# First four tiles mixed on 64x64 fourths of TensorE, first-stage products in groups of two and four blocks over several tiles, first loads issued from three queues

## The chip, the cores and the metric

The kernel runs on one core of a Trainium2 chip. The metric is the time of one execution on the device in microseconds (us). A core has five engines with queues of their own, each strictly in order, that meet only at semaphores: TensorE (PE in the profile, with PEld for its weight loads), VectorE (DVE), ScalarE (ACT), GpSimd (POOL) and SyncE (SP), which here only issues transfers. ACT and POOL can issue transfers too. PSUM, the memory that TensorE writes, cannot be read by POOL.

## The reference, cut to what matters

x is 32 x 64 x 1024 in f32. There are two layers, each a mix of the 64 channels of every batch entry by a matrix picked from a table, and then a 1024 x 1024 product over the last axis:

```
W = weights[condition]                      # 32 matrices of 64 x 64, picked from 16
y = einsum('bct,bcd->bdt', x, W)            # the mix over channels
x = x + y @ (w + (ternary(w) - w)) + b      # layer 0; ternary(w) = (|w| < 0.05 ? 0 : sign(w)) * mean|w| of a column
y = einsum('bct,bcd->bdt', x, weights1[condition])
x = x + y @ dequantized(q).T + bias + 4 * (y @ A.T) @ B.T     # layer 1; 4-bit levels, a scale for each 64
```

The output is x after both layers.

## The kernel before

**Tiles.** Two batch entries make a tile of 128 rows (2 x 64 channels) by 1024 columns: 16 tiles, `g` = 0 to 15 in layer 0, and the same 16 again as `g` = 16 to 31 in layer 1. The 1024 columns are 8 blocks `k` of 128 (`KB`), or two halves `n` of 512 (`BANK`).

**Work on a tile in layer 0.** PE mixes and turns the tile in one step, with x as the stationary operand: block k of x (128 rows by 128 columns) against the tile's two 64 x 64 matrices, which stand in `mix` as a block-diagonal 128 x 128 (`mixed(g)`), or on fourths of the array, 64 x 64 each, which skips the zero corners (`mixed_batches(g)`, tiles 4 to 15). The result goes to the PSUM tensor `xT` or, for tiles 1 and 3, to the banks 2 and 3 of `acc`. ACT rounds it into a high part (`high_x(g, h)`, tensor `hh` or `h23`, semaphore `s_hh`) and DVE takes the rest as a low part (`low_x(g, h)`, `hl` or `h23`, `s_hl`). PE then multiplies both parts by the ternary signs `T0` and accumulates 8 blocks x 2 parts into a bank of `acc` (`first(g, n, h)` for the tiles 0 to 3, in halves of four blocks, `main(g, n)` for the tiles 4 to 15). DVE scales the bank by the column means (`leave_y`, tensor `ys`), and POOL adds it to x (`result_half`, `result`), after `add_bias`. `ys` has four places, so `leave_y(q)` waits until POOL has finished `result_half(q - 4)` (`s_res0`).

**The signs.** For each of 16 pieces (n, k) of the first weight, 128 x 512, the signs are made either by ACT (`signs`, into `spare`, then `absolute` in place) with one DVE instruction (`ternary`), or by two DVE instructions (`ternary` of the blocks 0, 1, 4 and 6 of the first half), after which ACT still does `absolute`. `s_T0` counts the finished pieces. POOL adds up the absolute values of 8 pieces for each half with 7 additions, in the order of `ABS` (`sums(0, ...)`: 2, 3, 0, 1, 5, 4, 7, 6; then `sums(1, ...)`: 0 to 7). PE spreads each sum with a product of ones (`column_sums(n)`) and ACT scales it (`colscale(n)`).

**What sets the order.** All orders are written out by hand, for each engine a list of calls. POOL's list starts with the two `sums`, then alternates `add_bias(g)` and `result_half`, with `weight(d)` (a part of layer 1's weights) in between. DVE and ACT make layer 1's weights meanwhile (`maxima`, `lines`), 16 pieces `d` spread over the tiles 4 to 15, which PE turns (`turn_w`). After tile 15 come 8 pairs of tiles of layer 1 (`product`, seven products for each pair).

**Loads.** SP issues nearly all. Each 64 x 64 matrix for `mix` is one transfer whose address is looked up in `tok`. ACT issues the second matrices of the tiles 0 to 2 and the pieces 0 and 2 of the weight; POOL issues none.

The lists that the change touches begin like this on PE and on ACT:

```
turn_b()  mixed(0)  mixed(1)  mixed(2)  first(0, 0, 0)  first(1, 0, 0)  mixed(3)
first(0, 0, 1)  first(1, 0, 1)  column_sums(0)  first(2, 0, 0) ...
```

```
high_x(0)  signs(0, 2)  absolute(0, 2)  signs(0, 3)  absolute(0, 3)  high_x(1)
absolute(0, 0)  absolute(0, 1)  high_x(2) ... absolute(0, 7)  high_x(3)  absolute(0, 6)  signs(1, 0) ...
```

## Time and profile before

| | before |
|---|---|
| median of 3 runs | 343.64 us (343.38 to 344.93) |
| the profiled execution, its own time | 344.56 us |
| its span (first to last instruction) | 342.5 us |
| PE busy | 332.4 us, 97% |
| DVE busy | 236.0 us, 69% |
| POOL busy | 245.0 us, 72% |
| ACT busy | 164.5 us, 48% |

The span runs over three stages: the start until `main(4, 0)` at 51.0 us, the tiles 4 to 15 of layer 0 until 170.8 us, and layer 1. All views below have their times in us from the start of the span, so the difference of 2.1 us between time and span lies outside of them. A matmul of f32 operands leaves two records in the trace, one of fp32r operands leaves one.

### The profile page before, as it was taken

The page shows a single profiled execution, that of the slowest core. Times are in us where ns is not written, and L with a number is a line of the kernel's source. Part 1 is how long each engine was busy: PE and PEld are TensorE (multiplying, and loading weights), DVE is VectorE, ACT ScalarE, POOL GpSimd, SP SyncE. Part 2 cuts the span into 40 slices and gives each one's busy share as a digit, 9 for nine tenths or more (in the row PEclk, how much of TensorE's full clock was granted, in tenths as well). Part 3 has the DMA queues.
Part 4 walks back from the last instruction along what each step waited for, and adds up shares of the span by engine and source line. Part 5 has one row for each costly group of instructions (what it writes and reads, how often), then busy time and mean ns, then how long its engine had stood idle before and what let it go on. Part 6 is the DMA issues. An engine that isn't in the chain of part 4 may idle for free.

```text
span 342.5 us, 8187 instructions
## 1 busy us (share of the span) xinstructions
PE 332.4 (97%) x3142; PEld 271.4 (79%) x3142; DVE 236.0 (69%) x356; ACT 164.5 (48%) x300; POOL 245.0 (72%) x160
## 2 busy tenths in 40 slices
PE   7999999989999999999799999999999999999996
PEld 6868778778888778887678888888888888888884
DVE  7787567899999999999999736346263462624623
ACT  1799357877897787788171403214032140411400
POOL 0298999998896896986578966766467664677642
PEclk9999999999999999999999999999999999999999
DMA  6894511644354245300100151412513124150302
GB/s 229 291 341 132 201 33 33 271 168 159 118 167 162 93 157 177 141 10 13 55 2 3 65 189 63 150 44 74 181 65 131 63 84 169 67 169 23 124 31 92
DMA packets 25800, 40.60 MB, mean 119 GB/s; under 512 B 7810, under 2 KB 16002, under 8 KB 25762
## 3 DMA queue, kind: packets, MB, share of 16 engines
q1 hardware_dynamic: 25090, 39.48, 33.3%
q10 hardware_dynamic: 672, 0.61, 0.5%
q8 instruction: 25, 0.41, 0.5%
q14 instruction: 13, 0.11, 0.1%
HBM read 25.40 MB, written 14.68 MB: 117 GB/s over the span
## 4 chain that ended last, share of the span: by engine, by line
PE 51%; DVE 20%; POOL 12%; issue 8%; ACT 4%; DMA 1%; SPq 1%; DVEq 0%; POOLq 0%; ACTq 0%
PE acc L1268 45%; POOL col_scale L631 4%; DVE hl L914 3%; DVE ys L941 3%; POOL x_first L604 3%; PE spare L1154 2%; PE xT L1154 2%; POOL x_first L611 2%; DVE side_n L953 2%; ACT spare L762 2%; DVE W L988 2%; DMA w_in<-in_L_ffn_w 1%; POOL side_p L638 1%; DVE side_p L953 1%; DVE side_n L956 1%
## 5 line engine op out<-in xcount | busy, mean ns | idle before, releaser
L1268 PE MATMUL acc<-W,hh 128*128 128x512 f32 x256 | 81.4, 389 | 0.0
L1228 PE MATMUL acc<-T,hh 128*128 128x512 f32 x192 | 76.5, 398 | 0.0
L1228 PE MATMUL acc<-T,hl 128*128 128x512 f32 x192 | 75.0, 391 | 0.0
L604 POOL TENSOR_TENSOR X<-X,bias 128x1024 f32<-128x1024 f32 x28 | 68.1, 2432 | 0.0
L762 ACT ACTIVATE spare<-q_raw 128x512 f32<-128x512 int32 x96 | 56.1, 599 | 20.2 <-DVE side_n L953 5.0
L1040 DVE TENSOR_TENSOR X<-X,acc 128x512 f32<-128x512 f32 x48 | 32.9, 685 | 36.7 <-PE acc L1268 28.9
L1268 PEld LDWEIGHTS acc<-W,hh 128*128 128x128 f32 x256 | 48.0, 188 | 10.0
L663 POOL TENSOR_TENSOR X<-X,ys 128x512 f32<-128x512 f32 x24 | 30.5, 1299 | 34.1 <-DVE ys L1029 34.1
L1268 PE MATMUL acc<-W,hl 128*128 128x512 f32 x128 | 49.8, 389 | 0.0
L797 ACT ACTIVATE hh<-xT 128x512 fp32r<-128x512 f32 x16 | 8.7, 595 | 77.6 <-PE xT L1154 77.6
L1228 PEld LDWEIGHTS acc<-T,hh 128*128 128x128 f32 x192 | 36.0, 188 | 8.0
L1228 PEld LDWEIGHTS acc<-T,hl 128*128 128x128 f32 x192 | 36.1, 188 | 7.3
L1029 DVE TENSOR_TENSOR ys<-acc,ys 128x512 f32<-128x512 f32 x16 | 11.0, 690 | 34.2 <-PE acc L1268 33.3
L617 POOL TENSOR_TENSOR X<-X,ys 128x1024 f32<-128x1024 f32 x12 | 29.3, 2438 | 2.8 <-DVE ys L941 2.7
L638 POOL TENSOR_TENSOR side_p<-side_p,side_n 128x512 f32<-128x512 f32 x16 | 20.8, 1299 | 13.4 <-DVE side_n L959 13.4
L1268 PEld LDWEIGHTS acc<-W,hl 128*128 128x128 f32 x128 | 24.0, 188 | 5.0
L654 POOL TENSOR_TENSOR side_S<-plain_sums,side_S 128x512 fp32r<-128x512 f32 x8 | 10.4, 1302 | 23.0 <-ACT side_S L814 23.0
L941 DVE TENSOR_TENSOR ys<-acc,col_scale 128x512 f32<-128x512 f32 x32 | 21.8, 683 | 3.7 <-POOL x_first L611 3.7
L1268 PE MATMUL acc<-W 128*128 128x512 f32 x96 | 24.0, 399 | 0.0
L1268 PE MATMUL acc<-W,side_S 128*128 128x512 f32 x96 | 23.2, 390 | 0.0
L1268 PE MATMUL acc<-W_T,W 128*128 128x512 f32 x96 | 23.1, 389 | 0.0
L654 POOL TENSOR_TENSOR hl<-plain_sums,hh 128x512 fp32r<-128x512 f32 x16 | 21.6, 1353 | 0.0
(98 smaller groups left out, 606.5 us busy)
## 6 DMA issues: line engine op xcount, KB each, us to landing
out<-X SPq DMA_DIRECT2D x22, 512.0 KB, 3.1
X<-in_x SPq DMA_DIRECT2D x12, 512.0 KB, 3.4
X<-out SPq DMA_DIRECT2D x12, 512.0 KB, 3.8
q_raw<-in_L_ffn_q_weight SPq DMA_DIRECT2D x16, 256.0 KB, 2.9
w_in<-in_L_ffn_w SPq DMA_DIRECT2D x14, 256.0 KB, 6.8
x_first<-in_x SPq DMA_DIRECT2D x4, 512.0 KB, 5.1
out<-x_first SPq DMA_DIRECT2D x4, 512.0 KB, 4.6
out<-X SPq DMA_DIRECT2D x4, 256.0 KB, 2.0
```

The lines of the kernel that those rows point to most:

```text
L604: pool.tensor_tensor(x_of(g), x_of(g), bias[:, :], ALU.add).then_inc(s_xb, 1)
L617: pool.tensor_tensor(x_of(g), x_of(g), ys[:, at:at + NH, :].rearrange("p a f -> p (a f)"), ALU.add).then_inc(s_res0, NH)
L631: pool.tensor_tensor(col_scale[:, cols], col_scale[:, cols], w_raw(ABS[n][j], n), ALU.add).then_inc(s_sum, 1)
L638: pool.tensor_tensor(lev, lev, side_n[:, :], ALU.subtract).then_inc(s_lev, 1)
L654: pool.tensor_tensor(side(o, 1).rearrange("p b c -> p (b c)"), plain(i), side(o, 0).rearrange("p b c -> p (b c)").bitcast(F32), ALU.subtra ...
L663: pool.tensor_tensor(t, t, sum_of(which), ALU.add).then_inc(s_sum2, 1)
L762: act.activation(dst, q_raw[:, d % QS, :, :].rearrange("p o i -> p (o i)"), ACT.Copy, scale=slope, bias=offset).then_inc(s_line, 1)
L941: dve.tensor_tensor(ys[:, q % F, :], acc[:, bank_of(q), :], col_scale[:, n * BANK:(n + 1) * BANK], ALU.mult).then_inc(s_ys, 1)
L1040: dve.tensor_tensor(t, t, bank, ALU.add).then_inc(s_take, 1)
L1154: mm = pe.matmul(turned(g, h)[c * C:(c + 1) * C, k, rows], x_of(g)[rows, at:at + C], mix[rows, g % NM, rows], start=True, stop=True)
L1228: mm = pe.matmul(acc[:, bank_of(q), :], a[:, k, :], T0[:, n, k, :], start=(k == 0 and j == 0), stop=(k == KB - 1 and j == 1))
L1268: mm = pe.matmul(acc[:, bank, :], a[:, k, :], w1(part, c, k), start=(k == 0 and j == 0), stop=(k == HB - 1 and j == len(terms) - 1))
```

## The change

It reworks the lists of the start; everything from `main(4, 0)` on is the same.

1. The tiles 0 to 3 are mixed by `mixed_batches` too; tile 1 goes to the banks 2 and 3 of `acc`, the tiles 0, 2 and 3 to `xT`. The semaphore `s_xT` then rises by 2 at the end of a tile, not by 1 at each half. `high_x` and `low_x` work on columns for each batch entry instead of on blocks.
2. `first(g, n, start, stop)` takes a range of blocks, and PE's list interleaves ranges of 2 and 4 blocks of the tiles 0 to 2.
3. `idle(products)`: 7 products of the identity ahead of `turn_b` instead of 5, 4 after it, and 2 ahead of tile 1.
4. The second half of `loraB` is copied by ACT instead of DVE; ACT does `high_x(1)` ahead of `signs(0, 3)`, DVE does `low_x(1)` ahead of `ternary(0, 2)` and `low_x(2)` ahead of `ternary(0, 4)`.
5. POOL issues the weight pieces 0 and 1 and the four matrices of the tiles 2 and 3 (with semaphores of their own) ahead of its sums; ACT issues only the second matrices of the tiles 0 and 1; SP the rest.

```diff
-    WARM = 5
+    WARM = 7
@@ turned, batch
-            if g in (1, 3):
-                return acc[:, 2 + h, :].rearrange("p (b c) -> p b c", b=HB)
+            if g == 1:
+                return acc[:, 2 + s, :].rearrange("p (k c) -> p k c", k=KB)
@@ sync
             load_condition(sp, 0, 0)
             load_condition(sp, 1, 0)
+            load_weights(sp, 2, 0)
             load_x(2)
-            load_condition(sp, 2, 0)
-            load_weights(sp, 1, 0)
             load_weights(sp, 3, 0)
-            load_condition(sp, 3, 0)
             load_weights(sp, 4, 0)
+            load_weights(sp, 5, 0)
             load_x(3)
-            load_condition(sp, 3, 1)
-            load_weights(sp, 5, 0)
@@ gpsimd
+            load_weights(pool, 0, 0)
+            load_weights(pool, 1, 0)
+            pool.wait_ge(s_tok, 16)
+            pool.wait_ge(s_fill, 1)
+            for g in (2, 3):
+                for s in range(2):
+                    load_condition(pool, g, s)
             sums(0, 1, KB)
             sums(1, 1, KB)
@@ scalar
             load_condition(act, 0, 1)
-            load_weights(act, 0, 0)
             load_condition(act, 1, 1)
-            load_weights(act, 2, 0)
-            load_condition(act, 2, 1)
+            act.wait_ge(s_bT, 2)
+            act.activation(lora_columns(1), lora_turned(1), ACT.Copy).then_inc(s_loraB, 1)
             high_x(0, 0)
             high_x(0, 1)
             signs(0, 2)
             absolute(0, 2)
+            high_x(1, 0)
+            high_x(1, 1)
             signs(0, 3)
             absolute(0, 3)
-            high_x(1, 0)
-            high_x(1, 1)
@@ vector
+            dve.wait_ge(s_bT, 1)
+            dve.tensor_copy(lora_columns(0), lora_turned(0)).then_inc(s_loraB, 1)
             ternary(0, 0)
             low_x(0, 0)
             low_x(0, 1)
             ternary(0, 1)
+            low_x(1, 0)
+            low_x(1, 1)
             ternary(0, 2)
             ternary(0, 3)
-            low_x(1, 0)
-            low_x(1, 1)
+            low_x(2, 0)
+            low_x(2, 1)
             ternary(0, 4)
-            low_x(2, 0)
             ternary(0, 5)
-            low_x(2, 1)
@@ tensor
-            def first(g, n, h):
+            def first(g, n, start, stop):
 
                 q = n * F + g
-                if h == 0:
+                if start == 0:
                     bank_free(pe, q)
                     if q < NH:
-                        pe.wait_ge(s_loraB, q + 1)
-                    if g == 2:
-                        pe.wait_ge(s_hl, NH * F)
-                pe.wait_ge(s_hl, NH * g + h + 1)
-                for k in range(h * HB, (h + 1) * HB):
+                        pe.wait_ge(s_loraB, NH)
+                    pe.wait_ge(s_hl, NH * max(g + 1, 2 if q in (2, 3) else 0))
+                for k in range(start, stop):
                     pe.wait_ge(s_T0, n * KB + k + 1)
...
+            idle(WARM)
             turn_b()
-            mixed(0)
-            mixed(1)
-            mixed(2)
-            first(0, 0, 0)
-            first(1, 0, 0)
-            mixed(3)
-            first(0, 0, 1)
-            first(1, 0, 1)
+            idle(4)
+            mixed_batches(0)
+            idle(2)
+            mixed_batches(1)
+            first(0, 0, 0, 2)
+            first(1, 0, 0, 2)
+            mixed_batches(2)
+            first(0, 0, 2, 4)
+            first(1, 0, 2, 4)
+            first(2, 0, 0, 4)
+            first(0, 0, 4, 6)
+            mixed_batches(3)
+            first(1, 0, 4, 6)
+            first(2, 0, 4, 6)
+            first(0, 0, 6, KB)
+            first(1, 0, 6, KB)
+            first(2, 0, 6, KB)
+            first(3, 0, 0, HB)
             column_sums(0)
-            first(2, 0, 0)
-            first(2, 0, 1)
-            first(3, 0, 0)
-            first(3, 0, 1)
-            first(0, 1, 0)
-            first(0, 1, 1)
-            first(1, 1, 0)
+            first(3, 0, HB, KB)
+            first(0, 1, 0, HB)
+            first(1, 1, 0, HB)
+            first(0, 1, HB, KB)
+            first(1, 1, HB, KB)
             column_sums(1)
```

On PE, from `turn_b` (b_wide) on, this stood before, where `s_hl` counts low parts, `s_T0` finished sign pieces, and tile 0 multiplies four blocks in a row:

```order
L1284 MATMUL acc<-ident,b_wide 128x128 x7
L1139 MATMUL xT<-mix,x_first 128x128 [waits s_x00,s_mix0]
L1139 MATMUL xT<-mix,x_first 128x128 x7
L1139 MATMUL acc<-mix,x_first 128x128 [waits s_x01,s_mix1]
L1139 MATMUL acc<-mix,x_first 128x128 x7
L1139 MATMUL xT<-mix,x_first 128x128 [waits s_hl,s_x02,s_mix2]
L1139 MATMUL xT<-mix,x_first 128x128 x7
L1216 MATMUL acc<-T,hh 128x512 [waits s_T0,s_hl,s_loraB]
```

And this stands there now, up to the mixing of tile 2:

```order
L1299 MATMUL acc<-ident 128x128 x4
L1169 MATMUL xT<-mix,x_first 64x64 [waits s_x00,s_mix0]
L1169 MATMUL xT<-mix,x_first 64x64 x31
L1299 MATMUL acc<-ident 128x128 x2
L1169 MATMUL acc<-mix,x_first 64x64 [waits s_x01,s_mix1]
L1169 MATMUL acc<-mix,x_first 64x64 x31
L1211 MATMUL acc<-T,hh 128x512 [waits s_T0,s_hl,s_loraB]
L1211 MATMUL acc<-T,hl 128x512
L1211 MATMUL acc<-T,hh 128x512 [waits s_T0]
L1211 MATMUL acc<-T,hl 128x512
L1211 MATMUL acc<-T,hh 128x512 [waits s_T0,s_hl,s_loraB]
```

The mixing of tile 2 has moved behind two blocks of products of each of the tiles 0 and 1.

On ACT, from the high parts of tile 0 (`hh<-xT`) on, before:

```order
L723 ACTIVATE hh<-xT 128x512 [waits s_xT] x2
L730 ACTIVATE spare<-w_in 128x512 [waits s_T0,s_win2]
L736 ACTIVATE w_in<-w_in 128x512 [waits s_sign]
L730 ACTIVATE spare<-w_in 128x512 [waits s_T0,s_win3]
L736 ACTIVATE w_in<-w_in 128x512 [waits s_sign]
L723 ACTIVATE hh<-acc 128x512 [waits s_xT] x2
```

And now, where the signs of piece 3 (`s_win3`), whose absolute value is the second that POOL's sums wait for, stand behind the high parts of tile 1 (`hh<-acc`):

```order
L739 ACTIVATE hh<-xT 128x8x64 [waits s_xT] x2
L746 ACTIVATE spare<-w_in 128x512 [waits s_T0,s_win2]
L752 ACTIVATE w_in<-w_in 128x512 [waits s_sign]
L739 ACTIVATE hh<-acc 128x8x64 [waits s_xT] x2
L746 ACTIVATE spare<-w_in 128x512 [waits s_T0,s_win3]
L752 ACTIVATE w_in<-w_in 128x512 [waits s_sign]
```

On POOL, ahead of the first sum, stand now two weight loads and four matrices, of which the first is shown; before, the sums followed the identity directly:

```order
L489 DMA w_in<-in_L_ffn_w 128x512 x2
L481 TENSOR_LOAD tok [waits s_fill,s_tok]
L481 ISA x2
L483 ISA
L483 DMA mix<-in_L_cond_weights 64x64
```

## Rows read from the trace of the kernel before

**Rows 1.** Page, busy time by engine, and granted TensorE clock in 40 slices.
```profile
PE 332.4 (97%) x3142; PEld 271.4 (79%) x3142; DVE 236.0 (69%) x356; ACT 164.5 (48%) x300; POOL 245.0 (72%) x160
PEclk9999999999999999999999999999999999999999
```

**Rows 2.** Chain that ended last, in order of time: start, length, what.
```profile
6.82 5.10 DMA w_in<-in_L_ffn_w
...
14.10 0.63 ACT w_in L736
...
16.30 1.31 POOL col_scale L631
...
64.95 1.27 POOL side_p L638
66.24 0.63 ACT side_n L762
```

**Rows 3.** Timeline of POOL: start, length, line, what, idle before and releaser.
```profile
14.81 1.29 POOL L627 TENSOR_TENSOR col_scale<-w_in 128x512 f32<-128x512 f32 x1 [13.33 <-ACT w_in L736]
...
24.83 1.28 POOL L627 TENSOR_TENSOR col_scale<-w_in 128x512 f32<-128x512 f32 x1
...
33.45 2.10 POOL L631 TENSOR_TENSOR col_scale<-col_scale,w_in 128x512 f32<-128x512 f32 x1
35.51 2.41 POOL L604 TENSOR_TENSOR x_first<-x_first,bias 128x1024 f32<-128x1024 f32 x1
...
51.53 2.55 POOL L611 TENSOR_TENSOR x_first<-x_first,ys 128x512 f32<-128x512 f32 x2
```

**Rows 4.** Timeline of DVE, same columns.
```profile
11.95 0.69 DVE L929 TENSOR_SCALAR spare<-w_in 128x512 f32<-128x512 f32 x1 [0.39 <-DMA w_in<-in_L_ffn_w]
...
15.36 1.28 DVE L918 TENSOR_TENSOR hl<-acc,hh 128x512 fp32r<-128x512 f32 x2
...
33.14 1.25 DVE L1083 TENSOR_TENSOR loraA<-a_in,loraA 64x1024 fp32r<-64x1024 f32 x1 [0.26 <-ACT loraA L872]
...
52.95 0.69 DVE L941 TENSOR_TENSOR ys<-acc,col_scale 128x512 f32<-128x512 f32 x1 [3.66 <-POOL x_first L611]
...
67.39 0.69 DVE L953 SCALAR_TENSOR_TENSOR side_n<-side_n,spare 128x512 f32<-128x512 f32 x1 [0.83 <-ACT spare L762]
```

**Rows 5.** Busy time in 51 to 171 us; then PE's timeline at its longest wait there.
```profile
51.00:171.00 120.00, 115.91 (x1238) 93.35 (x1234) 111.37 (x170) 90.64 (x169) 99.33 (x60) 1.00 0.36 123
...
164.82 0.63 PE L1296 MATMUL acc<-ident,side_p 128*128 128x128 f32 x4 [1.86 <-DVE W_sums L978]
```

**Rows 6.** Timeline of TensorE's weight loads at the start.
```profile
1.53 2.21 PEld L1303 LDWEIGHTS acc<-ident 128*128 128x128 f32 x10 [1.53 <-POOL ident L667]
4.52 1.57 PEld L1284 LDWEIGHTS acc<-ident,b_wide 128*128 128x128 f32 x8 [0.78 <-DVE b_wide L1054]
6.42 3.48 PEld L1139 LDWEIGHTS xT<-mix,x_first 128*128 128x128 f32 x16 [0.34 <-DMA mix<-in_L_cond_weights]
...
11.96 1.87 PEld L1139 LDWEIGHTS xT<-mix,x_first 128*128 128x128 f32 x16
```

**Rows 7.** Timeline of PE: column sums 0; tile 5 mixed on fourths, then tile 4.
```profile
24.82 1.12 PE L1277 MATMUL xT<-col_scale,ones 128*128 128x512 f32 x2
25.38 7.86 PE L1216 MATMUL acc<-T,h 128*128 128x512 f32 x32
...
49.90 1.16 PE L1172 MATMUL xT<-mix,X 64*64 64x64 f32 x64
50.99 0.50 PE L1228 MATMUL acc<-T,hh 128*128 128x512 f32 x1
```

**Rows 8.** Timeline of ACT.
```profile
14.63 1.07 ACT L723 ACTIVATE hh<-acc 128x512 fp32r<-128x512 f32 x2
...
21.81 0.63 ACT L736 ACTIVATE w_in<-w_in 128x512 f32<-128x512 f32 x1
22.33 0.60 ACT L730 ACTIVATE spare<-w_in 128x512 f32<-128x512 f32 x1
...
26.96 0.58 ACT L740 ACTIVATE col_scale<-xT 128x512 f32<-128x512 f32 x1
```

**Rows 9.** Timeline of SP's queue, ACT's queue and DVE in the first microseconds.
```profile
3.08 0.58 SPq L467 DMA_DIRECT2D mix<-in_L_cond_weights  x1
4.45 0.47 SPq L467 DMA_DIRECT2D mix<-in_L_cond_weights  x1
...
2.79 0.91 DVE L1044 MEMSET a_in<- 128x1024 f32 x1 [0.16 <-DVE ones L1044]
```

74 lines of the change are left out of this document (30 added, 44 removed).

## Prediction

> **What bounds the kernel now.** The page comes first. PE is busy for 97% of the span at the full granted clock [rows 1], which invites the reading that every microsecond taken from PE is gained. The chain that ended last says otherwise for the first half: it leaves the start with a weight transfer, DVE and ACT, and enters POOL's first sums at about 16.3 us; it stays on POOL until 66.2 us and then on ACT and DVE [rows 2]. POOL's timeline shows why. Its first sum starts at 14.81, after a wait of 13.33 for ACT's `absolute`; from then on one instruction follows another: 14 sums at 1.44 us from start to start ((24.83 - 14.81)/7 = 1.43), the last one 2.10 long, then from 35.51 the pairs of `add_bias` and `result_half`, up to `result_half(3)`, the first of the two at 51.53 [rows 3]. DVE waits 3.66 us for exactly that one, at 52.95, and later only 0.83 at 67.39 [rows 4]; from 51 to 171 it is busy 111.4 of 120 us while PE, busy 115.9, waits 1.86 for DVE at 164.82 [rows 5]. So PE has some 4 us of idle time in that stretch, and it is DVE, released at 52.95 by POOL, that sets the end of layer 0. The rest is PE's own and is not touched. The question for the change is therefore when POOL finishes the second sums (35.51 before), not when PE reaches `main(4, 0)` (50.99 before [rows 7]).
>
> **The change, step by step.** Times are positions in the trace.
>
> *Tile 0 mixed, t0.* The 5 warm-up products take 0.44 each (2.21/5), `turn_b` 1.57 [rows 6]. Seven end at 1.53 + 7 x 0.44 = 4.6, which closes the pause ahead of `turn_b` (b_wide was ready at 4.5) and costs 0.1; `turn_b` ends at 6.2. A product of this size takes 0.44 at first (3.48/8) and 0.23 later (1.87/8) [rows 6], the two levels of the clock (1.2 and 2.4 GHz), although the page grants the full clock throughout [rows 1]. Before, the change of rate lies inside tile 1, between 10 and 12 us, and PE had paused at 3.7 to 4.5 and at 6.1 to 6.4. Now neither pause exists, so I let the rate change at about 7: four idle products end at 7.5. A tile on fourths takes 1.09 (49.90 to 50.99 [rows 7], whatever the change of shape costs included) against 1.9 to 3.5 whole. The matrices and x had landed by 6.42, where PE waited for them [rows 6]; with two more 256 KB loads in flight I allow 7.5. So t0 = 8.6. Bounds: 7.5 (6.42 + 1.1, rate changed early) and 10.2 (idle until 8.0, the tile twice as long).
>
> *The first signs.* `high_x(0)` 1.07 [rows 8], DVE's low parts end at t0 + 2.0, `ternary(0, 1)` needs 1.4 (two of 0.69 [rows 4]), so two pieces are signed at 12.0; before, this step waited for its weight until 11.95 and was done at 13.4. `signs(0, 3)` and `absolute(0, 3)` take 1.3 and POOL could start at 13.4, 1.4 us earlier than before.
>
> *The new waits.* `low_x(1)` now follows (1.2, a pair is 1.28 [rows 4]): 13.2. PE's list has `first(1, 0, 0, 2)` ahead of tile 2, so tile 2 is mixed from 13.2 + 0.9 = 14.1 to 15.2. Its high parts end at 16.4 and its low parts, which DVE now does ahead of `ternary(0, 4)`, at 17.2: DVE stands still from 14.4 to 16.0. `ternary(0, 4)` and `(0, 5)` end at 18.65 and 19.25. PE needs both for `first(0, 0, 4, 6)`, which stands ahead of tile 3: tile 3 is mixed from 20.1 to 21.2, and `high_x(3)`, ahead of `absolute(0, 6)` on ACT, ends at 22.3. `absolute(0, 6)` ends at 22.9, against 22.44 before (21.81 + 0.63), and `signs(1, 0)` starts at 22.85 against 22.33 [rows 8]. The lead of 1.4 us is a lag of 0.5 here: what tile 3's mixing gates on ACT has been put behind DVE's signs.
>
> *Second sums.* Each sign and absolute of the second half costs ACT 1.155 (four from 22.33 to 26.96 [rows 8]). `absolute(1, 1)` ends at 25.2, POOL's second sums start at 25.3 (24.83 before). Then ACT comes to `colscale(0)` at 27.5. PE's `column_sums(0)` stands behind 28 products of 0.2275 (7.86 for 32 gives 0.24 with the last one's own length; starts are 0.2275 apart) after tile 3: 27.6, ready at 28.2 with half of the 1.12 for the two passes. Before, it was done at 25.4, ahead of ACT's 26.96 [rows 7, 8]. ACT waits 0.75, the absolute of the fifth piece ends at 30.1, POOL would have wanted it at 29.6, and the last sum starts at 34.45. It ends at 35.75 if it takes the usual 1.30 and at 36.55 if it takes 2.10 as the last one did [rows 3] beside DVE's `loraA` correction (33.14, 1.25 long [rows 4]), which now falls on it again. Against 35.51 that is +0.2 to +1.0; I take +0.6.
>
> A rule bears on which. By the Trainium skill (SBUF — State Buffer, Who interferes with whom) a DVE instruction with two inputs in SBUF and a reading GpSimd instruction exclude each other, and whoever starts first keeps the ports. The trace agrees: DVE's correction starts first and ends at 33.14 + 1.25 = 34.39, and the sum beside it ends 1.16 later. By it POOL, starting 0.1 us ahead here, would take 1.30, DVE would pay, and the sum would be +0.2; by the row it is +1.0.
>
> *Loads on POOL.* No row shows POOL issuing. Nearest are SP's: a matrix with its look-up every 1.37 (3.08 to 4.45) and about 0.5 for a plain one [rows 9]: 2 x 0.5 + 4 x 1.37 = 6.5, done at 8.0. At twice that it is done at 14.5. Seven sums need 10.1 and the second sums cannot start before 25.3, so POOL may start as late as 15.2 at no cost; the loads are hidden in both cases. At three times, POOL would start at 21 and end near 42. SP and ACT shed four look-ups and two weight loads between them; this brings the later pieces earlier, but only piece 1 (0.39 [rows 4]) and, shortly, piece 2 had been waited for, and the new lists reach both later than they land.
>
> *After the sums.* POOL's list is unchanged and every input of it is ready earlier than needed, so the +0.6 goes to DVE at 52.95, on to 164.8 and to the end. PE reaches `main(4, 0)` at about 47.5: four tiles on fourths save about 5, eight idle products and its waits until 20 give back the rest. The 3.4 us go into longer waits for DVE.
>
> Sum: span 342.5 + 0.6 = 343.1. The profiled execution took 344.56, 0.9 above the median of the runs; against that median (343.64) the forecast is 344.2.
>
> **Rivals.** *PE bounds after all.* Then the 3.4 us of its lead arrive at the end: 340.2. For it: 97%. Against: DVE's 111 of 120 busy us and PE's wait at 164.82 [rows 5], and DVE can't move without POOL. A part of this case is also that I have a wait of the start too long, so that POOL ends 2 us earlier: 341.6. Together 0.17.
>
> *The rate of TensorE changes no earlier than before.* t0 = 10.2, tile 1 is mixed at 11.9, `low_x(1)` ends at 14.9 instead of 13.2, and every step behind it moves by 1.7: 345.9. For it: the page can't tell when it changes; against: PE has no pause. It decides from t0 = 9.7 on (over half a percent slower). 0.14.
>
> *POOL's own loads land late.* Piece 0 must be there by 7.9, or `low_x(0)` waits for `ternary(0, 0)` (1.4). Were POOL held back until DVE's memsets end at 3.70 [rows 9] and the load took the 5.10 of piece 1's [rows 2], it would land at 8.8 to 9.3: +1.0 to +1.4 on every step, 345.4. 0.11.
> The Trainium skill (DMA: Bandwidth & Descriptors, SWDGE vs HWDGE vs iDMA) speaks for this rival: transfers from GpSimd have their descriptors made in software, and a DVE instruction that holds the shared ports starves it. No row here shows it.
>
> *Forecast,* 0.58: POOL's end moves by -0.3 (t0 = 7.6) to +1.2.
>
> **Numbers.** Half a percent, 1.7 us, is about what a measurement here tells from no change. Faster by more: 0.17, the first rival. Slower by more: most of the second and over half of the third, and a tail of the forecast: 0.22. Same: 0.61. The range 341.5 to 346.3 leaves out the better half of the first rival and the ends of the slow ones; the forecast's own range is 343.3 to 344.9.
>
> **What would show it.** Right: POOL's first sum near 13.4 but its second sums at 25.3 and `add_bias(0)` near 36; ACT waiting for PE ahead of `colscale(0)`; DVE idle ahead of tile 2's low parts, near 15; PE's `main(4, 0)` near 47.5 with more idle time from 51 to 171; DVE's wait at 52.95 longer, its end at 53.5. Wrong: `add_bias(0)` before 34; PE's products at 0.44 beyond 9; a first sum after 15.2; or a DVE that no longer waits for POOL at 53.

## Result and the profile after

| | before | changed |
|---|---|---|
| time, median of 5 runs | 343.96 us (343.38 to 345.14) | 348.09 us (347.06 to 348.70) |
| profiled execution: time, span | 344.56, 342.5 us | 348.48, 346.8 us |
| mean granted TensorE clock in it | 0.999 | 0.990 |

The changed kernel is 4.1 us slower by the medians. By the means it takes 1.0107 times as long (95% interval 1.0073 to 1.0140), which is 3.7 us. The forecast of 344.2, and its range up to 346.3, are missed on the slow side.

First TensorE's weight loads, in the timeline of the changed kernel (as in [rows 6]; columns of all timelines are start, length, engine, line, what, and idle before with its releaser):

```profile
5.90 0.97 PEld L1299 LDWEIGHTS acc<-ident 128*128 128x128 f32 x8
8.56 1.02 PEld L1169 LDWEIGHTS xT<-mix,x_first 64*64 64x64 f32 x64 [1.69 <-DMA mix<-in_L_cond_weights]
9.66 0.52 PEld L1299 LDWEIGHTS acc<-ident 128*128 128x128 f32 x4
```

Its products (as in [rows 7]):

```profile
15.44 1.16 PE L1169 MATMUL xT<-mix,x_first 64*64 64x64 f32 x64
...
21.59 1.16 PE L1169 MATMUL xT<-mix,x_first 64*64 64x64 f32 x64
...
29.17 1.02 PE L1272 MATMUL xT<-col_scale,ones 128*128 128x512 f32 x2
```

ACT (as in [rows 8]):

```profile
22.82 1.09 ACT L739 ACTIVATE h<-xT 128x512 fp32r<-128x512 f32 x2 [0.95 <-PE xT L1169]
23.79 0.63 ACT L752 ACTIVATE w_in<-w_in 128x512 f32<-128x512 f32 x1
24.31 0.60 ACT L746 ACTIVATE spare<-w_in 128x512 f32<-128x512 f32 x1
...
30.22 0.60 ACT L756 ACTIVATE col_scale<-xT 128x512 f32<-128x512 f32 x1 [1.19 <-PE xT L1272]
```

PE has its full rate early (the 4 idle products behind `turn_b`, 8 records, in 0.97 us), but then waits 1.69 us for the matrix of tile 0, and tile 0 is mixed at 9.66. The chain that ended last shows that matrix from its issue by SP to its landing at 8.53 (start, length, what):

```profile
3.23 5.30 DMA mix<-in_L_cond_weights
```
Tile 2 is mixed from 15.44, tile 3 from 21.59, the signs of the second half start at 24.31, and ACT waits 1.19 us for the first column sums.

POOL of the changed kernel (as in [rows 3]):

```profile
14.48 1.29 POOL L640 TENSOR_TENSOR col_scale<-w_in 128x512 f32<-128x512 f32 x1 [6.69 <-ACT w_in L752]
...
26.81 1.29 POOL L640 TENSOR_TENSOR col_scale<-w_in 128x512 f32<-128x512 f32 x1 [1.01 <-ACT w_in L752]
...
32.06 5.62 POOL L644 TENSOR_TENSOR col_scale<-col_scale,w_in 128x512 f32<-128x512 f32 x4 [1.10 <-ACT w_in L752]
37.64 3.37 POOL L617 TENSOR_TENSOR x_first<-x_first,bias 128x1024 f32<-128x1024 f32 x1
```

DVE (as in [rows 4]):

```profile
17.30 1.29 DVE L928 TENSOR_TENSOR h<-xT,h 128x512 fp32r<-128x512 f32 x2 [1.87 <-ACT h L739]
...
36.42 2.33 DVE L1090 TENSOR_TENSOR loraA<-a_in,loraA 64x1024 fp32r<-64x1024 f32 x1 [0.26 <-ACT loraA L887]
...
56.01 0.69 DVE L950 TENSOR_TENSOR ys<-acc,col_scale 128x512 f32<-128x512 f32 x1 [4.78 <-POOL x_first L624]
```

POOL starts its second sums at 26.81 (24.83 before) and `add_bias(0)` at 37.64 (35.51), which takes 3.37 us instead of 2.41. DVE is released at 56.01 instead of 52.95 [rows 4]: 3.06 us later. The parts add up: 1.98 (start of the second sums) + 0.15 (their length) + 0.96 (the longer `add_bias(0)`) = 3.09. PE reaches `main(4, 0)` at 50.76, where the prediction had 47.5 and before it was 50.99, so PE has next to no lead.

The rest of the 4.3 us of span shows in PE's later timeline:

```profile
56.85 1.09 PE L1291 MATMUL acc<-ident,side_p 128*128 128x128 f32 x4 [2.17 <-DVE ys L950]
...
167.82 0.63 PE L1291 MATMUL acc<-ident,side_p 128*128 128x128 f32 x4 [1.83 <-DVE W_sums L987]
```

and in windows (window, its length, busy PE, PEld, DVE, ACT, POOL, granted clock, DMA share, GB/s):

```profile
58.00:60.00 2.00, 2.00 (x6) 1.52 (x6) 1.79 (x3) 1.48 (x3) 2.00 (x2) 0.50 0.04 8
166.00:168.00 2.00, 0.18 (x2) 0.21 (x3) 2.00 (x4) 0.00 (x0) 1.95 (x1) 1.00 0.54 173
168.00:170.00 2.00, 1.91 (x61) 1.54 (x62) 2.00 (x3) 0.60 (x1) 2.00 (x2) 0.83 0.04 9
170.00:172.00 2.00, 2.00 (x24) 1.59 (x19) 2.00 (x3) 0.60 (x1) 0.72 (x1) 0.50 0.00 0
172.00:174.00 2.00, 2.00 (x9) 1.60 (x8) 2.00 (x4) 0.00 (x0) 0.00 (x0) 0.82 0.00 0
```

The release at 167.82 is 3.00 later than the 164.82 of before [rows 5], the same shift as DVE's at 56. Behind PE's waits of 2.17 and 1.83 us the granted clock is 0.50, the lower of the two levels (1.2 against 2.4 GHz). At 58 PE isn't the bound. At 170 it is, and there it costs 1.2 us more (below).

### The profile page after: what moved, and what is told of

Read it like the earlier page. It is cut to its first block, busy times and chain, and to the rows that moved or that the text cites. A ratio compares the mean times of both kernels' runs of the same rounds, so it can differ in the third digit from the quotient of the medians.

```text
span 346.8 us, 8598 instructions
## 1 busy us (share of the span) xinstructions
PE 332.4 (96%) x3350; PEld 271.0 (78%) x3350; DVE 236.6 (68%) x355; ACT 165.8 (48%) x301; POOL 248.3 (72%) x166
## 4 chain that ended last, share of the span: by engine, by line
PE 56%; DVE 20%; POOL 9%; issue 8%; ACT 4%; DMA 2%; SPq 1%; DVEq 0%; POOLq 0%
PE acc L1263 44%; PE acc L1211 4%; DVE hl L928 4%; POOL x_first L617 3%; DVE ys L950 3%; PE spare L1149 2%; PE xT L1149 2%; POOL x_first L624 2%; DVE side_n L962 2%; ACT spare L778 2%; DVE W L997 2%; DMA mix<-in_L_cond_weights 2%; POOL side_p L651 1%; DVE side_p L962 1%; PE acc L1223 1%
## 5 line engine op out<-in xcount | busy, mean ns | idle before, releaser
L1223 PE MATMUL acc<-T,hh 128*128 128x512 f32 x192 | 77.9, 406 | 0.0
L1223 PE MATMUL acc<-T,hl 128*128 128x512 f32 x192 | 76.1, 396 | 0.0
L778 ACT ACTIVATE spare<-q_raw 128x512 f32<-128x512 int32 x96 | 56.2, 599 | 24.2 <-DVE side_n L962 8.5
L1223 PEld LDWEIGHTS acc<-T,hh 128*128 128x128 f32 x192 | 36.9, 192 | 8.3
L1223 PEld LDWEIGHTS acc<-T,hl 128*128 128x128 f32 x192 | 36.9, 192 | 7.6
```

The lines of the kernel that those rows point to most:

```text
L778: act.activation(dst, q_raw[:, d % QS, :, :].rearrange("p o i -> p (o i)"), ACT.Copy, scale=slope, bias=offset).then_inc(s_line, 1)
L1223: mm = pe.matmul(acc[:, bank_of(q), :], a[:, k, :], T0[:, n, k, :], start=(k == 0 and j == 0), stop=(k == KB - 1 and j == 1))
```

## The experiments

My theory after the result: DVE's release at 56 sets the time, and it is late through tile 0's matrix, through places in the lists, and through one collision of POOL with DVE; the clock at 168 adds to it. The rivals are named in each expectation. The medians below are of 6 to 12 runs. The ratios, of means, are to the kernel before, which was run beside them and had medians of 344.34 to 344.48. "Faster than the changed kernel" is against its median of 348.09. That one was measured beside a kernel before of 343.96, some 0.4 us lower, and the medians also move with how many runs have the clock's fall, so these gains are good to about half a microsecond.

**One law for all profiles.** In each profiled execution I read three things: the start of the `leave_y` that waits for `result_half(3)`, whether the granted clock falls between 160 and 174, and the span.

```
kernel          release  span   clock falls at 164-172  span - release
best2            49.88   339.7   no     289.8
before_pe_sum    51.07   341.9   yes    290.8
best1            51.45   341.5   no     290.1
fourths_only     52.09   342.8   yes    290.7
before           52.95   342.5   no     289.6
order_warm       53.83   343.4   no     289.6
pe_sum           54.07   343.7   no     289.6
colsum_early     54.29   343.8   no     289.5
order_colsum     54.41   345.3   yes    290.9
loads_only       54.53   344.1   no     289.6
w0_act           54.56   344.2   no     289.6
x1_late          55.34   345.0   no     289.7
idle_last        55.74   345.3   no     289.6
tile2_code       55.88   346.6   yes    290.7
after            56.01   346.8   yes    290.8
loads_back       57.25   346.8   no     289.6
tile2_early      59.08   348.6   no     289.5
```

Over 9 us of release the span follows one to one, 289.6 above it, or 290.8 where the clock fell. Only at the earliest releases does a little remain (best2: 0.2, best1: 0.5). Up to the end of layer 0 PE doesn't bound; `pe_sum` and `before_pe_sum` below, which move work from POOL to PE, are the test of it. The law also prices the clock's fall at 1.2 us, and shows that it isn't the change's own: `before_pe_sum` and `fourths_only` have it too.

**x1_late: the second x tile behind tile 0's matrix.**
```diff
-            load_x(1)
             sp.wait_ge(s_tok, 16)
             sp.wait_ge(s_fill, 1)
             load_condition(sp, 0, 0)
+            load_x(1)
```


> The changed kernel with SP's list turned in one place: the second x tile is loaded behind the look-up and matrix of tile 0 instead of ahead of it. Theory (a transfer in front of the matrix made the start late): in the trace of the changed kernel tile 0's matrix needed 5.30 us from SP's issue at 3.23 to landing, with 1.5 MB of x and weights issued ahead of it on three queues. With 0.5 MB fewer ahead of it, it lands 1 to 2 us earlier; tile 0 is mixed by about 8.6 instead of 9.66, every step up to POOL's second sums moves by about -1.0, DVE's release at 56.01 too, and the time by 1.0 to 1.3 us (347.0 against 348.1); more, up to 2.5, if the clock of TensorE then stays up at 168. Rival (the order of waits between 12 and 26 us sets the second sums, whatever the start does): below 0.4 us. Second rival: x of tile 1 lands after 10.3, so that tile 1 waits and the gain is given back.

347.72 us (1.0100, 1.0079 to 1.0120). Tile 0 is mixed from 7.84, against 8.57 in the changed kernel's profile. But this place varies between executions of one and the same start: 7.92 (`colsum_early`), 8.05 (`pe_sum`), 8.07 (`order_colsum`), 8.27 (`idle_last`), 8.57 (`order_warm`). The 0.4 us that the median gained is within this spread, and the forecast of 1.0 to 1.3 is missed. At most a small part of the delay is x ahead of the matrix.

**loads_back: the loads as before, the rest changed.**
```diff
-            load_weights(pool, 0, 0)
-            load_weights(pool, 1, 0)
...
-                    load_condition(pool, g, s)
...
             load_condition(act, 0, 1)
+            load_weights(act, 0, 0)
             load_condition(act, 1, 1)
+            load_weights(act, 2, 0)
+            load_condition(act, 2, 1)
```
SP's list is that of the kernel before too.

> The changed kernel with its first loads divided between SP and ACT as in the kernel before, and none on POOL; everything else as changed. Theory: the matrix of tile 0 lands by 7.5 again and tile 0 is mixed by 8.6, but weight piece 1 is back behind five others on SP, and before it was waited for until 11.95, so that two pieces are signed at 13.4 instead of 13.04. The two cancel: within 0.7 us of the changed kernel. Rival (POOL's loads are the cause of the loss): 3 to 4 us faster, near 344. Rival (the loads on POOL are what still helps): 1 us slower or more.

348.76 us (1.0129, 1.0105 to 1.0153), 0.7 above the changed kernel. The theory holds as a sum, at the edge: tile 0 is mixed from 7.74 with no wait (PE itself was late there, with its four idle products in 1.42 us instead of 1.06), but tile 2, which now stands behind products that need piece 1, only from 16.09, and DVE waits 3.32 us for its high parts. The new lists need the new loads.

**loads_only: the loads alone, on the kernel before.** Its edit is the inverse of the last one, on the kernel before.

> The kernel before the change with the first loads divided as in the changed one (weight pieces 0 and 1 and the matrices of tiles 2 and 3 issued by POOL), nothing else. Theory: piece 1 is there when DVE wants it (it waited until 11.95), which gives 0.4 us, and the matrix of tile 0 lands behind 0.5 MB more, up to 1 us later than 6.4, which takes up to 1: DVE's release at 52.6 to 53.6, 344.0 to 345.2. Rival (the loads are the loss): release at 54 or later, 346. Rival (the loads are the gain of the change): release before 52, 343.

346.32 us (1.0054, 1.0034 to 1.0075): 1.9 slower than before, above the 344.0 to 345.2 of the theory. PE's timeline:

```profile
8.50 3.55 PE L1148 MATMUL xT<-mix,x_first 128*128 128x128 f32 x16 [2.43 <-DMA mix<-in_L_cond_weights]
```
The matrix comes 2.1 us later than the 6.42 of [rows 6], and the products behind the wait run at half rate (the clock is 0.50 from 10 to 12). DVE's release is at 54.53. Both are what the rival "the loads are the loss" named (54 or later, 346), and not my theory.

**w0_act: only weight piece 0 back from POOL to ACT.**
```diff
             load_condition(act, 0, 1)
+            load_weights(act, 0, 0)
             load_condition(act, 1, 1)
...
-            load_weights(pool, 0, 0)
             load_weights(pool, 1, 0)
```


> The changed kernel with weight piece 0 issued by ACT behind its first matrix, as before the change, instead of by POOL at the start; POOL keeps piece 1 and the matrices of tiles 2 and 3. Theory (POOL's 0.5 MB at 1.84 lie ahead of tile 0's matrix): with half of it the matrix lands near 6.8 to 7.2, as it did at 6.75 in the version of before with piece 1 on POOL, and is then no longer waited for; tile 0 is mixed by 8.0 to 8.9 instead of 9.66 and DVE released 0.7 to 1.2 earlier, 347.0 against 348.1. Piece 0 may land at 8.5 to 9 in its place, where it is just in time (DVE's first low parts came at 10.43). Rival (the matrix is late through its own issue or the number of queues): no earlier than 7.9, and no gain.

346.06 us (1.0062, 1.0039 to 1.0085): 2.0 faster than the changed kernel by the medians, 1.5 by the means. PE's timeline:

```profile
7.11 1.16 PE L1169 MATMUL xT<-mix,x_first 64*64 64x64 f32 x64
```
and DVE's:
```profile
54.56 0.69 DVE L950 TENSOR_TENSOR ys<-acc,col_scale 128x512 f32<-128x512 f32 x1 [4.76 <-POOL x_first L624]
```
POOL's second sums:
```profile
25.37 1.29 POOL L640 TENSOR_TENSOR col_scale<-w_in 128x512 f32<-128x512 f32 x1 [1.02 <-ACT w_in L751]
```
PE no longer waits for the matrix. Tile 0 is mixed 1.46 earlier, the second sums start 1.44 earlier, and DVE's release comes 1.45 earlier, more than the 0.7 to 1.2 expected: the start is passed on one to one. How much of the 1.46 is the load's is less certain. The ten profiles with both pieces on POOL have tile 0 from 7.84 to 8.70, so one load of 256 KB that POOL issued at 1.84 held tile 0 back by 0.7 to 1.6 us.

And POOL's early issue bought nothing for piece 0 itself. The chain of `w0_act` shows it issued by ACT at 3.59:
```profile
3.59 3.93 DMA w_in<-in_L_ffn_w
```
DVE had it at 7.55; issued by POOL at 1.84, it had it at 7.50. The edit changes the queue and the time of issue together, so whether the queue or the place ahead of the matrix did the harm isn't separated.

**colsum_early: the first column sums 12 products earlier** (the expectations say 20; the edit passes 4 products of tile 2 and 8 of tile 3).
```diff
             first(1, 0, 6, KB)
+            column_sums(0)
             first(2, 0, 6, KB)
-            first(3, 0, 0, HB)
-            column_sums(0)
-            first(3, 0, HB, KB)
+            first(3, 0, 0, KB)
```


> The changed kernel with PE's product for the first column sums placed 20 products earlier (ahead of the last fourth of tile 2's first half instead of in the middle of tile 3's). Theory: ACT's wait of 1.19 us for it at 30.22 and POOL's wait of 1.10 at 32.06 go; POOL's second sums still start at 26.8 and end at 36.6 instead of 37.64, so DVE is released at about 55.0 and the time falls by 1.0, or by up to 2.4 if TensorE's clock then stays up at 168. Rival (POOL's end is not what sets the time): no change within 0.3 us.

346.51 us (1.0068, 1.0044 to 1.0092), 1.6 faster. Both waits are gone. In the profiled execution tile 0 came 0.65 earlier; the release is 1.72 earlier (54.29), so 1.07 is the edit's. It isn't all the wait's. POOL:
```profile
36.83 2.38 POOL L617 TENSOR_TENSOR x_first<-x_first,bias 128x1024 f32<-128x1024 f32 x1
```
`add_bias(0)` has its 2.4 us again, since DVE's correction now starts at 34.44, beside the sums, and the last six of these take 9.30 us as they did before the change. So the wait had put POOL's sums back by about 0.96, and had moved the collision from the sums (0.8) to `add_bias(0)` (0.96).

**order_colsum: four places of the lists.**
```diff
+            mixed_batches(3)
             first(0, 0, 4, 6)
-            mixed_batches(3)
...
+            absolute(0, 6)
             high_x(3, 0)
             high_x(3, 1)
-            absolute(0, 6)
...
+            ternary(0, 4)
             low_x(2, 0)
             low_x(2, 1)
-            ternary(0, 4)
```
These are PE's, ACT's and DVE's lists; the column sums are moved as in colsum_early.

> The changed kernel with four places of its lists turned: the first column sums 20 products earlier; the signs of piece 4 ahead of tile 2's low parts on DVE; the absolute of piece 6 ahead of tile 3's high parts on ACT; tile 3 mixed ahead of the products of pieces 4 and 5 on PE. Theory (the wait of 1.87 us for tile 2's high parts and tile 3's late mixing put the second sums back): ACT gets to the first signs of the second half at about 22.2 instead of 24.31, POOL is then bound by its own first sums and starts the second at about 24.7 instead of 26.8, DVE is released at 53.0 instead of 56.0, and the time is 344.0 to 344.7, 3.4 to 4.1 us below the changed kernel and equal to the one before. Rival (the start, with tile 0's matrix and the loads, is what counts): no better than the version with the column sums alone, 346.5. Second rival (clock falls after PE's waits account for the loss): the wait at 56 stays long, and under 1 us comes back beyond 346.5.

345.12 us (1.0029, 1.0011 to 1.0047), 3.0 faster than the changed kernel, and 0.4 above the theory's range. Its 12 runs fall apart: the seven with a mean granted clock of 0.998 or more took 344.35 to 345.26, the five with 0.985 to 0.990 took 345.94 to 347.31. The profiled one has 0.985, and its windows show where:

```profile
12.00:14.00 2.00, 0.92 (x4) 0.49 (x4) 2.00 (x4) 1.85 (x5) 0.02 (x1) 1.00 1.06 417
14.00:16.00 2.00, 2.00 (x24) 1.21 (x27) 1.97 (x4) 0.94 (x2) 1.86 (x2) 0.55 1.03 393
16.00:18.00 2.00, 2.00 (x58) 1.84 (x51) 0.25 (x1) 0.46 (x1) 1.86 (x2) 0.59 1.06 407
```
and PE's timeline what it did there:
```profile
15.48 1.99 PE L1169 MATMUL xT<-mix,x_first 64*64 64x64 f32 x64
```
PE was busy for 0.92 of 2 us from 12 to 14, and then tile 2 was mixed at half rate (1.99 us against 1.16), here on the path: the second sums started at 26.26 in this execution, not at 24.7. At full clock, in `order_warm`'s profile, they started at 25.66.

**order_warm: the same with idle products in PE's waits near 12 and 13.**
```diff
-            first(0, 0, 0, 2)
+            first(0, 0, 0, 1)
+            filler(3)
+            first(0, 0, 1, 2)
+            filler(3)
             first(1, 0, 0, 2)
```


> The version with four places of the lists turned (345.12, its runs at a full mean clock 344.4 to 345.0, at 0.985 to 0.99 346 to 347), with 3 idle products before each of the two places where PE waits near 12 and 13 us. Theory (the clock fell at 14 to 18 because PE stood still there): no run below a mean clock of 0.99, the profiled one at 1.00 from 12 to 20, tile 2 mixed in 1.16 us, and a median of 344.4 to 344.9. Rival (the fall has another cause, such as what came before 10 us): runs at 0.985 come as often, median 345.1 or more.

344.84 us (1.0019, 1.0001 to 1.0038). The profiled execution has a clock of 1.00 from 8 to 22, but tile 2 still took 1.48 us, and 4 of 12 runs have 0.990 to 0.995. No run is at 0.985, where two were. The median is in the range of my theory, but 0.3 us doesn't tell it from the rival.

**idle_last: 8 idle products in PE's last wait.**
```diff
+                            if d == ND - 1:
+                                bank_free(pe, NH * g + n + 1)
+                                for _ in range(8):
+                                    pe.matmul(acc[:, bank_of(NH * g + n + 1), 0:P], ident[:, :],
+                                              ident[:, :], start=True, stop=True)
                             turn_w(d)
```


> The changed kernel with 8 idle products (128 x 128) into a free bank in PE's wait of 1.83 us ahead of the turning of the last weight piece (167.82). Nothing else differs. Theory (the clock fell because PE stood still there): the granted clock stays 1.00 from 168 to 174, the products of 170.45 to 172.74 take half their time, and the time falls by 1.2 to 1.5 us. Rival (the clock's fall has another cause, or comes anyway): no change, or up to 0.2 us slower through the products themselves.

346.95 us (1.0081, 1.0058 to 1.0104), 1.1 faster. Windows:

```profile
166.00:168.00 2.00, 1.96 (x19) 1.79 (x17) 2.00 (x5) 0.00 (x0) 2.00 (x1) 1.00 0.29 86
170.00:172.00 2.00, 2.00 (x10) 1.61 (x10) 2.00 (x3) 0.47 (x1) 0.46 (x1) 1.00 0.00 0
```
PE is busy in the wait, and the clock stays; 0.3 us of the gain is an earlier start (release at 55.74). Of the changed kernel's five runs, three had a mean clock of 0.990 (348.09 to 348.70) and two 0.995 or 1.000 (347.06, 347.09); here one of six was at 0.989 (348.51). That speaks for the theory, weakly. But a wait of as long as 1.83 to 1.86 us there left the clock up in the profiles of before, `x1_late`, `colsum_early`, `w0_act` and others, and let it fall in `order_colsum` and `before_pe_sum`, so the wait alone doesn't decide it.

**pe_sum and before_pe_sum: POOL's last second sum left to PE**, in the changed kernel and in the one before.
```diff
-            sums(1, 1, KB)
+            sums(1, 1, KB - 1)
...
-                pe.matmul(flat(n), ones[:, :], col_scale[:, n * BANK:(n + 1) * BANK],
-                          start=True, stop=True).then_inc(s_colsum, 1)
+                mm = pe.matmul(flat(n), ones[:, :], col_scale[:, n * BANK:(n + 1) * BANK],
+                               start=True, stop=n not in (1,))
+                if n in (1,):
+                    pe.wait_ge(s_abs, (n + 1) * KB)
+                    mm = pe.matmul(flat(n), ones[:, :], w_raw(ABS[n][KB - 1], n),
+                                   start=False, stop=True)
+                mm.then_inc(s_colsum, 1)
```


> The changed kernel with the last of POOL's seven second sums left to PE: the second column sums are made of two products that add up, one over the six sums and one over the last absolute weights. The result is the same sum in another order. Theory (POOL's end sets DVE's release and so the time): add_bias(0) starts 1.4 us earlier, DVE is released at 54.6 instead of 56.0, and the time falls by 1.4 us, to 346.7; by up to 2.8 if the clock then stays up at 168. Rival (PE bounds after all): 0.45 us slower, by the two passes of PE that it adds.

> The kernel before the change, with the last of POOL's second sums left to PE in the same way. Theory: POOL's end moves from 35.51 to about 33.4 (the last sum took 2.10 beside DVE's correction, the one before it may now take that), DVE is released at 51.0 to 51.6 instead of 52.95, and the time falls by 1.4 to 2.0 us, to 342.5 to 343.1: faster than both kernels. Rival (PE, busy for 97% of the span, bounds there): 0.45 us slower. Between: PE's 4 us of waiting from 51 to 171 are partly used up, and the gain is under 1 us.

pe_sum: 345.46 us (1.0043, 1.0024 to 1.0061), 2.6 faster than the changed kernel; its release is at 54.07, 1.94 earlier, of which 0.52 is an earlier tile 0 and 1.42 the edit's, as forecast. The rest of the 2.6 goes with the clock, which six of its seven runs kept (a mean of 0.999 or 1.000). before_pe_sum: 343.32 us (0.9966, 0.9953 to 0.9978), 1.1 faster than before, with the release at 51.07, as forecast; part of the gain went to the clock at 164 in 5 of 12 runs (343.57 to 343.94 at 0.994 or 0.995 against 342.15 to 343.52). "PE bounds" would have been 0.45 slower in both. Less work on POOL and more on PE makes both kernels faster.

The collision of DVE's correction with POOL shows again, here in `pe_sum`; POOL:

```profile
35.75 2.40 POOL L617 TENSOR_TENSOR x_first<-x_first,bias 128x1024 f32<-128x1024 f32 x1
38.22 2.14 POOL L624 TENSOR_TENSOR x_first<-x_first,ys 128x512 f32<-128x512 f32 x1
```
and DVE:
```profile
35.97 3.26 DVE L1090 TENSOR_TENSOR loraA<-a_in,loraA 64x1024 fp32r<-64x1024 f32 x1 [0.27 <-ACT loraA L887]
```
DVE's correction takes 1.25 alone [rows 4]. Here it starts behind POOL's instruction and ends at 39.23, 1.08 after it; POOL's next one, begun at 38.22, takes 2.14 instead of 1.29. In the changed kernel it is 2.33 on DVE behind the last sum, and 3.37 instead of 2.41 on POOL's next. Whoever starts first keeps its time; the other waits, and DVE gets its turn ahead of POOL's next instruction. `w0_act`, `x1_late`, `idle_last` and `loads_back` show the same pair, 2.33 to 2.35 on DVE and 3.38 or 3.39 on `add_bias(0)`.

**fourths_only: only the mixing on fourths, on the kernel before.**
```diff
-                for k in range(KB):
-                    mm = pe.matmul(turned(g, k // HB)[:, k % HB, :], x_of(g)[:, k * P:(k + 1) * P],
-                                   mix[:, g % NM, :], start=True, stop=True)
-                    if k % HB == HB - 1:
-                        mm.then_inc(s_xT, 1)
+                for k in range(KB):
+                    for s in range(2):
+                        rows = slice(s * C, (s + 1) * C)
+                        for c in range(2):
+                            at = k * P + c * C
+                            mm = pe.matmul(batch(g, s)[c * C:(c + 1) * C, k, :], x_of(g)[rows, at:at + C],
+                                           mix[rows, g % NM, rows], start=True, stop=True)
+                mm.then_inc(s_xT, NH)
```
`high_x` and `low_x` take columns instead of blocks, and `first` waits for both low parts.

> The kernel before the change with one part of it alone: tiles 0 to 3 are mixed on fourths of the array. Loads, idle products and every list stay as before. Theory: low parts of tile 0 are ready at about 10 instead of 11.56, but DVE then waits for weight piece 1 until 11.95 as before; tiles 2 and 3 are mixed 0.8 us faster each, and little of that reaches ACT, which was busy. POOL's second sums start at 24.2 to 24.8 (24.83 before); the time is within 0.6 us of the kernel before, on the faster side. Rival (fourths make both halves of a tile wait for the whole, and this is the loss): 1 us slower or more.

344.17 us (0.9995, 0.9979 to 1.0011), as forecast: this part costs nothing, and gains nothing that can be measured. (The second sums, at 23.93, came a little ahead of the 24.2 expected.)

**tile2_early and tile2_code: tile 2 mixed ahead of the first products.**
```diff
+            mixed_batches(2)
             first(0, 0, 0, 2)
             first(1, 0, 0, 2)
-            mixed_batches(2)
```
DVE does `ternary(0, 4)` ahead of `low_x(2, 0)`, as above. tile2_code also has
```diff
-            idle(4)
+            idle(1)
             mixed_batches(0)
-            idle(2)
```


> The changed kernel with tile 2 mixed directly behind tile 1, ahead of the first products, as in the kernel before, and the signs of piece 4 ahead of tile 2's low parts on DVE. Theory (tile 2's place behind the first products makes ACT wait 1.23 and DVE 1.87 us for it): tile 2 is mixed by 13, ACT goes from absolute(0, 1) at 15.4 straight to its high parts, the first signs of the second half come at 22.5 instead of 24.31 and the second sums start at 25.0 instead of 26.8. The column sums stay late, so that ACT's wait for them grows and takes back 0.3 to 0.5. DVE is released at 54.3 to 54.8 instead of 56.0. In the runs so far the span was 289.6 above that release, or 290.8 where the clock fell at 168; the time is then 346.0 +- 0.4, or 1.2 more. Rival (the start alone counts): the release stays within 0.4 of 56, 347.5 or more.

349.54 us (1.0143, 1.0113 to 1.0173): my clearest miss, 1.5 slower where I expected 2 faster. PE's timeline:

```profile
11.99 1.15 PE L1169 MATMUL xT<-mix,x_first 64*64 64x64 f32 x60 [0.40 <-DVE hl L928]
16.15 0.33 PE L1169 MATMUL xT<-mix,x_first 64*64 64x64 f32 x4 [3.01 <-issue]
```
and, among the DMA queues in the window from 13 to 14 us (packets, MB, share of 16 engines):
```profile
q8 instruction: 1, 0.02, 6.0%
```
The counts are of records, two for a product: with 2 of tile 2's 32 products to go (the expectation below takes records for products) PE stood still for 3.01 us and waited for nothing that the profile names, while a transfer of instructions ran. But the same transfer stands in the same window of the changed kernel and of `order_colsum`, where PE never stood for 3 us, so its presence says little. Tile 3 was then mixed only from 24.61.

> The version with tile 2 mixed early, with 5 of PE's idle products fewer ahead of it (3 before tile 0, 2 before tile 1). In that version PE stood still from 13.14 to 16.15 with 60 of tile 2's 64 products done. Theory (PE ran out of instructions there, at a fixed place of its program): the stand comes again, but 5 products later, so that all 64 of tile 2's are done ahead of it and it falls into the first weight products; tile 2's high parts then start near 15.5, when ACT is free, instead of 16.53. Its end stays near 16. The time falls by 1 us or less. Rival (a wait that the trace doesn't name, on tile 2's data): the stand stays at the same product of tile 2.

346.99 us (1.0097, 1.0059 to 1.0135), 2.6 faster than tile2_early by five idle products fewer. In the profiled execution (348.32 us) the stand didn't come 5 products later; it didn't come at all. One of the six runs took 350.81, and whether it had the stand isn't known. In the profile PE waited 2.38 us ahead of tile 2, until 12.31, which the trace puts down to the load of x. So neither expectation holds. The stand goes with what is ahead of it, if one profile of each can show that; that the instructions were late is argued, not shown.

**best1 and best2: what gains, put together.** best1 is the kernel before with the edits of fourths_only, before_pe_sum and idle_last. best2 also has piece 1 taken from SP's list, and
```diff
+            load_weights(pool, 1, 0)
             sums(0, 1, KB)
```


> The kernel before the change with three parts: tiles 0 to 3 mixed on fourths, the last second sum of POOL left to PE, and 8 idle products in PE's last wait of layer 0. From the runs with one part each: fourths put DVE's release from 52.95 to 52.09, PE's sum put it to 51.07; together 50.3 to 50.8 if they add, span 289.6 more with the clock kept, time 341.6 to 342.1. Rival (PE bounds once DVE is released 2.5 us earlier): 342.5 to 343.3, no better than PE's sum alone (343.3).

> The same as the version with three parts (fourths, PE's sum, idle products in the last wait), and weight piece 1 issued by POOL at the start instead of by SP behind five others. In the runs DVE waited 0.4 to 0.7 us for that piece near 11. Theory: this wait goes and the release moves by -0.4 to -0.8 more: 341.0 to 341.6. Rival: the 256 KB lie ahead of tile 0's matrix, which lands later by as much, and nothing is gained or 0.5 us lost.

best1: 343.51 us (0.9964, 0.9950 to 0.9978), over the 341.6 to 342.1 expected and no better than PE's sum alone. Its release, 51.45, is later than `before_pe_sum`'s 51.07, so the gain was lost ahead of the release; only the 0.5 by which its span is above the law can be PE's. In its profile DVE waits for piece 1, and the fourths' lead is lost there:

```profile
11.23 0.69 DVE L921 TENSOR_SCALAR spare<-w_in 128x512 f32<-128x512 f32 x1 [1.12 <-DMA w_in<-in_L_ffn_w]
```
best2: 342.35 us (0.9939, 0.9922 to 0.9956), the fastest kernel here, 0.6% below before and 5.7 us below the changed one. DVE, best2:

```profile
49.88 0.69 DVE L933 TENSOR_TENSOR ys<-acc,col_scale 128x512 f32<-128x512 f32 x1 [1.57 <-POOL x_first L612]
```
With POOL loading piece 1 alone, DVE doesn't wait for it, and the release is 1.57 earlier than best1's, for the 0.4 to 0.8 expected (by the medians of the time it is 1.2). The rival's price is there too, but smaller: tile 0 starts at 6.75 instead of 6.18. The profiled execution took 341.55, as forecast; the median is 0.8 us above the forecast.

## Why the prediction was wrong

**What bounds** was right: POOL's end releases DVE, and DVE sets the end of layer 0. The rival "PE bounds" is out. The issues on POOL were rightly sized too: POOL was through with them at 7.8, for the 8.0 forecast.

Five terms were too small, and no single one explains the miss: the landing of tile 0's matrix (1.06), the steps behind it (0.45), ACT's wait for the column sums (0.4), the collision (0.96 where 0.4 was counted) and the clock (1.2 in an execution in which it falls). PE's forecast lead of 3.4 us didn't come either (`main(4, 0)` at 50.76, not 47.5), but nothing hung on it.

**The first step that failed is "The matrices and x had landed by 6.42 ...; with two more 256 KB loads in flight I allow 7.5".** They landed at 8.5 in the profiled execution, and t0 was 9.66, not 8.6. `w0_act` shows the cause, the load of piece 0 on POOL: without it t0 is 8.20, and what t0 gains the release and the span gain. Other executions of the same start had t0 down to 8.93, so a part of the 1.06 is spread. I had looked at POOL's loads only for their own landing (my third rival: DVE held for piece 0, which came in time at 7.50), not for what they push back on another queue. The rival on the clock reached almost this t0 (9.7 was its threshold) by another way, and that isn't what happened in the profiled execution: PE was at full rate from about 5 us. But a later change of rate does occur. In `pe_sum` the four idle products took 1.61 us, tile 0 started at 8.05 behind them, and PE waited for no matrix:

```profile
6.51 1.61 PE L1304 MATMUL acc<-ident 128*128 128x128 f32 x8
8.05 1.16 PE L1169 MATMUL xT<-mix,x_first 64*64 64x64 f32 x64
```

**The steps from t0 on** were right to half a microsecond: with t0 1.06 later I would have had POOL's first sum at 14.46 and the second sums at 26.4; they were at 14.48 and 26.81. `w0_act`, with t0 = 8.2, has 25.37 against the 24.9 that my steps give. Of these 0.45 us, 0.28 stand at tile 2 already (15.44 for 15.16, four products ahead of it in 1.10 us instead of 0.9), and the rest came by tile 3 (21.59 for 21.16). The places of the lists were the right suspects: the four turned places give back 3.0 us of the 4.1.

**"ACT waits 0.75"** was mis-sized: 1.19, which put POOL's sums back by 0.96; I had charged some 0.5 for it (the last sum at 34.45 instead of 33.9).

**The collision.** The second step that failed, a mechanism left out and not a size, is "POOL's list is unchanged and every input of it is ready earlier than needed, so the +0.6 goes to DVE": `add_bias(0)` had its inputs, and still took 3.37 us instead of 2.41. I took one loss of 0.8 or none on POOL's last sum and chose between a row and a rule. By the Trainium skill (SBUF — State Buffer, Who interferes with whom) the one that starts first keeps the ports. The trace agrees, with 2.33 us on DVE behind POOL's sum. But the trace shows more than the page states: DVE's turn comes ahead of POOL's next instruction, which lost 0.96. POOL pays in either case; my "+0.2" by the rule forgot this. Before, it paid 0.8 too, so the collision as such explains 0.2 us of the change, and the rest of the 0.96 replaces a loss that I had already counted.

**The clock.** "The rest is PE's own and is not touched" put this term at nothing, and no step had the fall at 168. It costs 1.2 us in an execution that has it, and three of the changed kernel's five had a mean clock of 0.990.

**The sum.** Release predicted +0.6, measured +3.06. The 2.5 between them: second sums at 26.81 instead of 25.3 (1.51, of it 1.06 from t0); their length as predicted (10.83 against 36.15 - 25.3 = 10.85), since the longer wait for the column sums and the collision that moved off them cancel; and the collision on `add_bias(0)`, 0.96. With the clock's 1.2 the span is 4.3 longer.

**Left open:** what decides whether the clock falls behind a wait of this length; the stand of 3.01 us; whether it is POOL's queue or only the place ahead of the matrix that delays it; and why the matrix lands anywhere from 7.84 to 8.70 with the same loads.

## What to carry to other kernels

A load given to an idle queue isn't free: ask which small transfer, already waited for, it will push back, and give that one the first place. When one engine's end sets the time, find the single instruction that hands it on; here one subtraction, the release, told the span of 16 of 17 profiles to 0.2 us once the clock's fall was known, and work taken from that engine paid even on a PE that was 97% busy. List places must be moved together with the loads that feed them: here the new loads with the old lists and the new lists with the old loads were both slower than the kernel before. And read the same place in several profiles before pricing a difference at it: the start of tile 0 varied by 0.9 us with the same loads.

## What the runs showed of the hardware

- One 256 KB load issued by POOL at 1.84 us delayed a 16 KB matrix, issued on SP's queue at 3.23, by 0.7 to 1.6 us (tile 0 starts at 7.84 to 8.70 in ten profiles with it, and at 7.11 in `w0_act`). The load itself was there no sooner than when ACT issued it at 3.59 (7.50 against 7.55). The Trainium skill (DMA: Bandwidth & Descriptors, SWDGE vs HWDGE vs iDMA) warns that DVE can lock GpSimd out of the memory where it puts its descriptors. No run here shows that: POOL's own load landed in time, and another queue's was late.
- Two DVE and POOL instructions on SBUF ran one behind the other, and the turns alternated: 3.26 us for 1.25, then 2.14 for 1.29.
- The granted clock went to 0.50 behind waits of PE of 1.8 to 2.2 us in some profiles (changed, `order_colsum`, `before_pe_sum`) and stayed at 1.00 behind equal waits in others (before, `w0_act`, the last wait of `x1_late`). Where PE bounds, it cost 1.2 us.
- PE stood still for 3.01 us with 30 of 32 like products done, waiting for nothing that the trace names.
